# Nine expert tiles placed between the last routing steps of an attention and mixture-of-experts kernel

## The reference

```python
h = layernorm(x) * (1 + ca) + sa              # modulation from silu(c) @ wmod
x = x + ga * attention(h)                     # 16 heads of 8, scores + q . rel_table[clip(j - i)]
h = layernorm(x) * (1 + cb) + sb
logits = silu(h @ rw1 + rb1) @ rw2 + rb2      # router, 128 -> 512 -> 8
k_logits, k_index = top_k(logits, 2); k_prob = softmax(k_logits)
for e in range(8):                            # experts, 128 -> 512 -> 128
    we = sum(where(k_index == e, k_prob, 0))
    out += we * (silu(h @ w1[e] + b1[e]) @ w2[e] + b2[e])
x = x + gb * out
```

## Time and profile before

| | us |
|---|---|
| median of 3 runs | 765.39 (762.88 to 766.69) |
| profiled execution, its own time | 765.92 |
| its span, first to last instruction | 764.2 |
| rounds 0 to 15, up to the last exponentials | 511.6 |
| from there to the first matmul of an expert tile | 58.1 |
| expert tiles, to the last scatter's issue | 162.8 |
| rest | 31.7 |

### The profile page before, as it was taken

How to read it: one execution, slowest core, us unless ns; L and a number is a source line. 1 busy time by engine, 2 the same in 40 slices (tenths; PEclk the granted TensorE clock), 3 DMA queues, 4 the chain that set the end, 5 groups by cost and what they waited for, 6 DMA issues and landing times. The chain is left out here.

```text
span 764.2 us, 17822 instructions
## 1 busy us (share of the span) xinstructions
PE 602.8 (79%) x4962; PEld 451.9 (59%) x4962; DVE 565.2 (74%) x1959; ACT 572.4 (75%) x1709; POOL 470.4 (62%) x576
## 2 busy tenths in 40 slices
PE   5478888888897988888888988886329999999820
PEld 3355566565665656655665655553218998989710
DVE  5887888889889888988888889854516666656524
ACT  2058989889898898898898898991018888988622
POOL 2633645865787778778778777746421655655634
PEclk9758989999999999999999999996559999999955
DMA  5888888787788878888887887920175888888456
GB/s 157 251 206 250 246 249 259 220 257 237 232 248 245 258 245 241 256 250 252 255 252 238 254 248 245 279 77 21 54 219 185 272 277 278 272 255 291 155 152 178
DMA packets 189430, 172.25 MB, mean 225 GB/s; under 512 B 18115, under 2 KB 175588, under 8 KB 189334
## 3 DMA queue, kind: packets, MB, share of 16 engines
q1 hardware_dynamic: 183494, 161.75, 69.9%
q0 software_dynamic: 4832, 8.44, 3.3%
q10 hardware_dynamic: 1008, 0.93, 0.4%
HBM read 97.94 MB, written 74.63 MB: 226 GB/s over the span
## 5 line engine op out<-in xcount | busy, mean ns | idle before, releaser
L583 ACT ACTIVATE P<-NS,nmax 128x256 f32<-128x256 f32 x512 | 253.9, 499 | 54.0 <-DVE nmax L1015 51.4
L1015 DVE CUSTOM_DVE_ANT_0 NS<-psS,bias 128x256 f32<-128x256 f32 x512 | 185.5, 418 | 1.9 <-PE psS L765 1.9
L966 DVE COPY stage<-psDist 128x768 f32<-128x768 f32 x125 | 119.0, 952 | 45.7 <-PE psDist L720 13.4
L783 PE MATMUL psT<-ident,P 128*128 128x128 f32 x1024 | 139.6, 280 | 10.6 <-ACT PT L594 9.7
L1309 POOL DMA_INDIRECT results_d<-y,row_u x87 | 86.4, 993 | 86.3 <-ACT y L1332 66.9
L783 PEld LDWEIGHTS psT<-ident,P 128*128 128x128 f32 x1024 | 117.3, 144 | 33.9 <-issue 17.0
L594 ACT ACTIVATE PT<-psT 128x512 f32<-128x512 f32 x256 | 135.4, 580 | 0.7 <-PE psT L783 0.7
L765 PE MATMUL psS<-Kst,Qst 32*128 32x256 f32 x512 | 66.2, 337 | 50.2 <-DVE nmax L1015 49.3
L1459 DVE TENSOR_TENSOR FL<-F,FH 128x384 fp32r<-128x384 f32 x116 | 62.0, 555 | 51.3 <-ACT FH L1346 51.3
L583 ACT ACTIVATION_READ_ACCUMULATOR P<-NS,nmax 128x1 f32 x512 | 96.9, 189 | 0.0
L765 PEld LDWEIGHTS psS<-Kst,Qst 32*128 32x128 f32 x512 | 39.3, 189 | 77.8 <-DVE nmax L1015 70.4
(11 more groups left out here) (235 smaller groups left out, 1286.1 us busy)
## 6 DMA issues: line engine op xcount, KB each, us to landing
dist_d<-stage SPq DMA_DIRECT2D x128, 384.0 KB, 3.2
bias<-dist_d SPq DMA_DIRECT2D x256, 192.0 KB, 3.4
wUp<-pairs_d SPq DMA_DIRECT2D x29, 512.0 KB, 4.6
wDown<-pairs_d SPq DMA_DIRECT2D x29, 512.0 KB
pairs_d<-pair SPq DMA_DIRECT2D x16, 512.0 KB, 3.5
x<-slots_d SPq DMA_DIRECT2D x29, 193.5 KB
raw<-in_L_ffn_w_dram SPq DMA_DIRECT2D x16, 256.0 KB, 4.2
y<-results_d SPq DMA_DIRECT2D x16, 256.0 KB, 5.0
```

The costliest lines, as they stand in the source:

```text
L583: act.activation(P[:, p % 2, h, q, :], NS[:, p % 2, h, q, :], ACT.Exp, scale=-1.0, bias=nmax[:, p % 2, k:k + 1], accum_out=lsum[:, b % 2, ...
L783: mm = pe.transpose(psT[:, h, S * k + 128 * q:S * k + 128 * q + 128], P[:, p % 2, h, q, 128 * k:128 * k + 128], ident[:])
L966: dve.tensor_copy(stage[:, p % STAGES, :, :, :], bank[:, :, 0:2 * RW].rearrange("p h (q c) -> p h q c", q=2)).then_inc(dist_out, 1)
L1015: dve.tensor_tensor_reduce(NS[:, p % 2, h, q, :], psS[:, h, S * q:S * q + S], bias[:, p, h, q, :], 1.0, 3e38, ALU.add, ALU.min, nmax[:, p ...
```

## The change

- Tables: M jobs and X jobs get other steps, "rank" another offset, and a new X job "tally" sums the counts of the first twelve batches in round 15. `weigh` is cut in halves that are put in seven of the eight steps (`W_SLOTS`).
- Order within a step: PE does the X job before `scores`. ACT takes its M jobs (y, nh) and the sums `lrow` before the exponentials. DVE multiplies the context in step 3 and before `put_out`. POOL begins a round with `normalise_again`, then `widen`, then `mix`.
- `choose` and `slots` are two steps later; rows of batches 10 and 11 are sent in round 15, 12 and 13 in round 17, 14 and 15 in round 19.
- Two tables of tiles: `plan_full` plans the first `FULL` = 9 tiles, which are full whatever the last four batches choose (6144 rows, at most 383 left over in each of eight experts), and `plan_rest` the other 20. The first part of SP's queue waits only for batches 0 to 11.
- The expert stage moves into the same loops: each tile is cut in five parts (`part`), and one part is put behind each step from (16, 1) to (19, 2), but for step 6. These are 23 parts. The rest follow in a plain loop, and from part 41 on they are tiles of the second table.
- ACT's and SP's `pad` come in step (19, 2) and between loads of tiles 6 and 7. `plan_rest` comes behind step (18, 7), ahead of the last "rank".
- `y` has ten buffers in place of two; the down product and the turned result have one PSUM bank each in place of two. The tiles of stage 2 lie where stage 1's lay.
- Tokens are numbered so that the final loads read 2048 contiguous bytes per partition. The exponential of the probabilities comes behind the last tile.
- The block is opened with `no_gpsimd_drain=True`.

```diff
-M_SLOTS = ((("q23", 1),), (("logits", -3), ("v", 1)), (("k01", 1),), (("k23", 1),),
+M_SLOTS = ((("q23", 1),), (("k01", 1),), (("k23", 1),), (("logits", -3), ("v", 1)),
            (("y", -1), ("nh", 2)), (("u01", -2),), (("u23", -2),), (("q01", 2),))
-X_SLOTS = ((), (), (("rows", -3),), (("turn", -2),), (("back", -2),), (), (("t", -1),), (("rank", -3),))
+X_SLOTS = ((), (("rank", -4),), (("turn", -2),), (("tally", 1 - B),), (("rows", -3),), (("back", -2),), (("t", -1),), ())
+W_SLOTS = ((2, (1,)), (3, (0,)), (3, (1,)), None, (0, (0, 1)), (1, (0,)), (1, (1,)), (2, (0,)))
...
+def parts_until(b, p):
+    steps = [k for k in range(PAIRS * (b - B) + p + 1) if k > 0 and k % PAIRS != 6 and k <= 2 * PAIRS + 10]
+    return len(steps)
...
-        block = ctx.enter_context(nc.Block())
+        block = ctx.enter_context(nc.Block(no_gpsimd_drain=True))
...
+            sp.wait_ge(planned, 1)
+            load_w(0, 0, wUp, up, 0, up_in)
+            for k in range(RINGS):
+                sp.wait_ge(sent[k], 16 * 4 * KNOWN // RINGS)
+            load_x(0)
...
+            for j in range(2, FULL + 1):
+                if j == FULL - 2:
...
+                    pad(sp, range(EXP // 2))
+                if j < FULL:
+                    load_x(j)
...
+            sp.wait_ge(planned, 2)
...
+            for k in range(RINGS):
+                sp.wait_ge(sent[k], 16 * 4 * B // RINGS)
+            sp.wait_ge(filled, 16 * (EXP + 1))
+            load_x(FULL)
...
@@ act, step
-                if b < B:
-                    exps(b, p)
-                if p == 2 and 0 < b <= B:
+                at = before(b, p)
+                if p == 3 and 0 < b <= B:
                     sums(b - 1)
-                at = before(b, p)
                 for name, of in M_OF.get(at, ()):
                     if name in BY_ACT:
                         act.wait_ge(m_full, M_DONE[at][0] + 1)
                         take(name, of)
+                if b < B:
+                    exps(b, p)
...
@@ act, part of a tile
+            def part(j, k):
+                if k < HK and j < JOBS:
+                    if k == 0:
+                        act.wait_ge(planned, 1 if j < FULL else 2)
+                        which[j] = of_tile(act, j)
+                    unit(j, k, which[j])
+                    if k == 1 and j + 1 < JOBS:
+                        split_x(j + 1)
+                    if k > 0:
+                        split_f(j, k - 1)
+                elif k == HK:
+                    if j < JOBS:
+                        split_f(j, HK - 1)
+                    if j >= 2:
+                        rows_out(j - 2)
...
+                    if (b, p) == (B + 3, 2):
+                        pad(act, range(EXP // 2, EXP))
+                    while n < parts_until(b, p):
+                        part(n // PARTS, n % PARTS)
+                        n += 1
...
@@ pe, step
                 later, after = shifted(b, p, AHEAD), shifted(b, p, 1)
-                if after[0] < B:
-                    scores(*after, later if later[0] < B else None, (b, p))
                 for name, of in X_OF.get((b, p), ()):
                     past(pe, dist_out, min(PAIRS * b + p + AHEAD, STEPS))
                     spare_taken(b, p)
                     extra(name, of)
...
+                if after[0] < B:
+                    scores(*after, later if later[0] < B else None, (b, p))
+                if W_SLOTS[p] and (0, 4) <= (b, p) <= (B, 2):
+                    g, parts = W_SLOTS[p]
+                    weigh(b - int(p < 4), g, parts)
...
                 elif name == "rows":
-                    pe.wait_ge(m_dve, so_far(M_DONE, r + 3, 1)[1])
+                    pe.wait_ge(m_dve, so_far(M_DONE, r + 3, 3)[1])
...
+            def part(j, k):
+                if k < HK and j < JOBS:
+                    go_up(j, k)
+                    if k == 1 and j + 1 < JOBS:
+                        turn_x(j + 1)
+                elif k == HK:
+                    if j >= 2:
+                        turn_y(j - 2)
+                    if 0 <= j - 1 < JOBS:
+                        go_down(j - 1)
...
+                    if (b, p) == (B, 1):
+                        turn_x(0)
...
@@ dve
+                    if (b, p) == (B + 2, 7):
+                        plan_rest()
+                    while n < parts_until(b, p):
+                        part(n // PARTS, n % PARTS)
+                        n += 1
```

More of the change, by code:

```diff
@@ L399, in _ @@
+            sp.wait_ge(stored, 16 * CHUNKS)
         @block.gpsimd
@@ L548, in _ @@
                     mix(b - 2, 0)
+                if b == B + 2:
+                    send_result(0)
+            for j in range(1, JOBS):
+                send_result(j)
+            for c in range(CHUNKS):
+                at = slice(CK * c, CK * c + CK)
+                pool.wait_ge(gated, c + 1)
+                pool.tensor_tensor(y2[:, at, :], y2[:, at, :], X[:, at, :], ALU.add).then_inc(added, 1)
         @block.scalar
@@ L1124, in step @@
                     variance(mean_r)
+                if p == 3 and 0 < b <= B:
+                    context(b - 1)
                 link_up(1)
@@ new lines, in jobs @@
+            def jobs(at, per, extra):
+                n = at.stop - at.start
+                then(dve.tensor_tensor(wide[:], rep(per[:], 1, EXP), until[:], ALU.mult))
+                then(dve.tensor_reduce(cum[:], wide[:], AX.X, ALU.add))
+                then(dve.tensor_tensor(gone[:, 0:n, :], rep(jobno[:, 0:n], 2, EXP), rep(cum[:], 1, n), ALU.is_ge))
+                then(dve.tensor_tensor(gone_t[:, 0:n, :], gone[:, 0:n, :], rep(extra, 1, n), ALU.mult))
+                dve.tensor_reduce(ex[:, 0:n], gone[:, 0:n, :], AX.X, ALU.add)
+                then(dve.tensor_reduce(first_f[:, 0:n], gone_t[:, 0:n, :], AX.X, ALU.add))
@@ L1146, in _ @@
+            n = 0
             for b in range(B + LAST):
@@ L1148, in _ @@
                     step(b, p)
-            dve.wait_ge(choice, 9 * B // 2)
-            dve.tensor_tensor(total[:], earlier[:, TT, :], earlier[:, 0, :], ALU.subtract).then_inc(totalled, 1)
-            then(dve.tensor_scalar(until[:], until[:], 0.0, None, ALU.is_ge))
-            dve.wait_ge(counted, 1)
-            dve.tensor_copy(cnt_u[:], psM[:, 0:EXP]).then_inc(table, 1)
-            then(dve.tensor_copy(cnt[:], psM[:, 0:EXP]))
-            then(dve.tensor_tensor(more[:], rep(cnt[:], 2, MOST), steps[:], ALU.is_gt))
```

687 lines of the change are left out of this document (349 added, 338 removed).

## The result

The changed kernel takes 740.15 us (median of its runs, 739.54 to 741.73) beside 764.42 for the kernel before on the same chip: a ratio of 0.9683, interval 0.9651 to 0.9715. That is 24.3 us less. 717 were forecast, 47 less, and the range ended at 740. The profiled execution took 740.75 us, its span is 738.7.

A forecast was written before the change was run, and what follows sets the result against it. Bound: in the rounds a ring of DVE's maxima, PE's products and DVE's copy through in-order queues, then a chain behind attention. 765.9 - 21 (rounds) - 21 (tail) - 5.7 (drain) = 718.2, taken as 717 us; range 692 to 740.

The forecast's parts named there:

- "rows", +1.1: Step 4 of a round: this X job, now ahead of the scores, waits for logitT and V; +1.1 us a round.
- y and nh taken ahead of the exponentials: the 0.98 us of step 6 goes: Step 6 of a round: ACT takes them earlier, so DVE's idling before its copy goes; -1.0 us a round.
- `choose` and `slots` fall on steps with takes of their own: +0.3: Rounds: moved two steps later, they meet steps that already have takes; +0.3 us a round.
- 23 parts lie on the chain: Tail before the last slots: tile parts worth 23.4 us, half assumed hidden in idle time; +12 us.
- `plan_rest`, +5.2: Tail: planning the second table stands ahead of the last ranks, with the wait for the count; +5.2 us.
- Table loads, +2.6: Tail: silu alternates with tanh, two loads of 1.28 us on the chain; +2.6 us, or 5.3 by the Trainium skill.
- The clock, -4: Tail: PE, at a clock of 0.61 before, idles less with parts between; 4 us off, 0 if it stays.
- The first tile late, +3.5: Tail, counted from A, the end of attention: PE stands waiting for tile 0's rows and weights; +3.5 us.
- The rows for tile 9, 20.2 us after the slots, "so they are hidden": Tail: rows needed until A+77, while the parts before them run until A+80.5, so no wait was expected.
- the rounds don't shorten: Rival: the wait of "rows" and a late POOL or ACT eat the rounds' saving; 738 us, chance 0.14.
- the tail gives nothing: Rival: parts and chain queue behind each other on three in-order queues; 738 us, chance 0.14.
- POOL as the bound: Rival: 92 scatters pace the expert stage if each takes from 2.0 us; 776 at 2.1 us, chance 0.03 with the like.

The follow-up runs named there:

- Experiment 6: Changed kernel with PE's job "rows" in step 4 waiting for the transposed logits alone, not for V: 738.66 us, ratio 0.9641.
- Experiment 4: Changed kernel with PE's M jobs of step 4 (y, nh) ahead of the weighing instead of behind it: 734.21 us, ratio 0.9608.
- experiment 5: Changed kernel with ACT taking y and nh behind the exponentials, as before the change: 739.49 us, ratio 0.9668.
- experiment 15: Changed kernel with `choose`'s nine operations spread over steps 5, 6, 7 and 0: 742.92 us, ratio 0.9707.
- 16: Changed kernel with M jobs first, "rows" on logits alone, tile 9's rows first, ACT's split first, `plan_rest` behind the slots, `choose` spread: 714.47 us, ratio 0.9363.
- experiment 1: Kernel before the change, with only the block opened with `no_gpsimd_drain=True`: 760.83 us, ratio 0.9946.
- Experiment 2: Changed kernel with no tile part between the routing steps, all 41 parts of the first table behind the last step: 742.48 us, ratio 0.9719.
- Experiment 7: Changed kernel with ACT's split ahead of the silu in the 23 parts between the rounds: 735.38 us, ratio 0.9594.
- experiment 12: Changed kernel with M jobs first, "rows" on logits alone, `choose` later, tile 9's rows first, ACT's split first, `plan_rest` behind the slots: 726.29 us, ratio 0.9483.
- experiment 8: Changed kernel with POOL splitting the piece of round 15 ahead of its sends: 739.98 us, ratio 0.9653.
- experiment 3: Changed kernel with tile 9's rows loaded ahead of two loads of weights in SP's queue: 732.80 us, ratio 0.9588.
- the ten kernels: The changed kernel and nine variants whose engines do the same from the end of attention (A) to the slots, which come at A + 61.2 to A + 68.2.
- experiment 13: Changed kernel with M jobs of step 4 ahead of the weighing and "rows" waiting for the logits alone: 732.33 us, ratio 0.9584.

## Why the prediction was wrong

Faster was right, and so was what bounds the kernel; the size is half. By its own steps:

- **Step 2 of the round, -1.3; "rows", +1.1, and the X jobs ahead of the scores, -0.7:** right. Step 2 went from 5.05 to 3.78; steps 3 and 4 together, which were to grow by 0.4, grew by 0.33 (4.02 and 3.33 to 3.17 and 4.51). So the miss of 0.8 us a round lies in steps 5 to 7: they were to give 0.7 and cost 0.1 more. Experiment 6 shows that 0.5 of "rows" is the wait for V, and that alone it is worth 0.29 us a round.
- **"y and nh taken ahead of the exponentials: the 0.98 us of step 6 goes", and a later start of ACT's exponentials "at nothing, up to 1 us if that cover is gone":** this step failed. The cover was gone: "rows" makes step 4 late on PE, the M jobs behind it and the weighing make nh late, and ACT waits 1.74 us with everything behind it. Step 6 gave 0.4 of 1.0. Experiment 4 gets it back (3.55), experiment 5 shows that ACT's order isn't what costs while nh is late. The forecast had weighed the two moves one by one, and not that one delays the other.
- **"`choose` and `slots` fall on steps with takes of their own: +0.3":** mis-sized where it falls, in step 5. The even step 5 is 1.0 us longer than the odd one, of it 0.97 a comparison that stands behind POOL's product; that is 0.5 on the mean of the rounds. That I had looked only at DVE's order when `choose` was moved, and not at what POOL does in those steps, is the omission. What the wait costs the whole round isn't shown: experiment 15 cuts it to 0.25 us and the round stays, and 16 gains 1.3 to 2.9 us in all, with overlapping intervals.
- **The sum of the rounds:** 0.77 us a round by the sums of rounds 3 and 13, against 1.6 forecast. Experiments 4 and 6 together bring it to 28.25 and the spread to 28.16: close to 28.1 was there to be had, with another order of PE's jobs and a shorter wait. Of the 0.8 us missed, these two edits explain 0.68.
- **Drain, -5.7:** right within what experiment 1 can tell.
- **"23 parts lie on the chain", "I take half: +12":** this step failed, and it is the large one of the tail. Experiment 2 measures 27.1 for them, 21.5 to 28.5 with the spread, about the 23.4 that I gave for none hidden. PE was idle 16 us in the stretch before, but a part is a round trip of PE, ACT and DVE in three in-order queues. DVE's 16.7 us of waiting for ACT's split up to the slots show an engine standing before its share of the tile with the chain's next link behind it. Experiment 7 takes 10.7 of these waits away and has the slots 3 to 10 us earlier, by ACT's order alone.
- **The rest of the sum up to the slots:** an error the other way. Experiment 2, with no part on the chain, leaves of the forecast's terms 37.9, 5.2 for `plan_rest` and up to 3.5 for the first tile, A + 43 to A + 47; it has A + 39.7. What made the rest of the chain shorter isn't shown. Without it the slots would have come later still.
- **`plan_rest`, +5.2:** measured 5.0, and experiment 12 takes 5.1 off. **Table loads, +2.6:** none came, so neither of the two prices given for them was put to the test. **The clock, -4:** it rose, from 0.61 to 0.80. What that gave isn't measured by itself, but the ten kernels give a scale: from 0.80 to 0.89 PE is busy for 6.1 us less and the slots come 7.0 earlier. **The first tile late, +3.5:** PE waits 1.15 us for its rows and has its first product at A + 7.0, for which 5.5 was forecast; experiment 8 shows no gain in having it earlier.
- **The rows for tile 9, 20.2 us after the slots, "so they are hidden":** the step that failed in the tail's second half. The queue was forgotten: SP has two loads of weights ahead of them that wait for a buffer. 5.7 us between tiles 8 and 9, 7.3 of the time by experiment 3.
- **The total:** 11.9 + 11.7 - 4.9 + 6.7 = 25.4 of the span's 25.5 where 47 were forecast: 9 us short in the rounds, 9 in the tail up to part 41, 5 behind it.
- **The rivals:** "the rounds don't shorten" and "the tail gives nothing" were each given 738 as if one or the other. The result is within 2.2 us of that, but neither happened: both parts gave about half, so the nearness is chance. It lies 0.15 us outside the range. POOL as the bound didn't come: the scatters of results take 984 ns in the mean.

What stays open: how much of the 27 us the order costs and how much the clock gives back; a variant in which DVE's half of the split stands behind the chain's link wasn't tried. What the granted clock in that stretch depends on isn't shown either: it lies between 0.79 and 0.89 in kernels that do the same there.

## What to carry to other kernels

Idle time of single engines didn't hide work here: 23 parts put "into the gaps" of a chain on in-order queues delayed it by about all that they are worth. Cost such work as a round trip with the chain behind it, and take "behind the chain" as the kernel to beat. When two things are moved in a round, follow the second with the first one's delay in place. And look at what stands ahead of a load in its queue before calling it hidden, and at what the neighbouring engine runs when two-input vector work is moved. A stretch of one profiled execution has a spread of its own, here 7 us in 65: look at the granted clock before giving such a difference to an edit.

## What the runs showed of the hardware

- A VectorE tensor-tensor operation of 0.42 us, both inputs in SBUF, that begins while GpSimd runs a product took until 0.28 us behind that product's end: 1.38 to 1.39 us in the changed kernel, and 1.15 behind the shorter product in experiment 13. GpSimd is held up too: its product L553, begun at 286.94 in experiment 13, took 1.45 us where it takes 1.27 in a round without `choose`.
- Tanh between silus brought no table load: one load of 1283 ns at 507.9 serves both until the exponential of the probabilities at 708.9.
- TensorE's granted clock was 0.61 in the chain before, near the lower of its two levels (1.2 of 2.4 GHz), with PE busy 22.0 of 37.9 us. With the parts in it, it was 0.80, with PE busy 46.0 of 66.8. In ten kernels that do the same there it was 0.79 to 0.89, and PE was busy 46.9 us at 0.80 and 40.8 at 0.89 (experiments 6 and 5) for the same matmuls. In the window of a steady round and from 600 to 700 it was 1.00.
